# Causal attention in a four-layer kernel: side units of the first stage issued behind the next probability-value piece

## The reference, cut to what matters

```
x = x + attn(layernorm(x))              # x: 8 batches x 1024 tokens x 256
q, k, v = x @ Wq, x @ Wk, x @ Wv        # 16 heads of 16 columns
scores = where(causal, q k^T, -inf) / sqrt(256)
out = softmax(scores) @ v               # per batch and head
```

## Time and profile before

| what | us |
|---|---|
| median of 3 runs (lowest, highest) | 4321.05 (4316.38, 4322.92) |
| the profiled execution, its own time | 4314.35 |
| its span in the trace | 4312.6 |
| PE busy | 4047.0 (94%) |
| DVE busy | 2816.3 (65%) |
| ACT busy | 2658.4 (62%) |
| POOL busy | 1553.8 (36%) |
| the steps of causal attention, from the first score piece on | 85.4 to 1282.1 of the span |

### The profile page before, as it was taken

How to read it: one execution, slowest core, us unless ns; L and a number is a source line. 1 busy time by engine, 2 the same in 40 slices (tenths; PEclk the granted TensorE clock), 3 DMA queues, 4 the chain that set the end, 5 groups by cost and what they waited for, 6 DMA issues and landing times. The chain is left out here.

```text
span 4312.6 us, 65428 instructions
## 1 busy us (share of the span) xinstructions
PE 4047.0 (94%) x23476; PEld 2363.6 (55%) x23476; DVE 2816.3 (65%) x5635; ACT 2658.4 (62%) x3262; POOL 1553.8 (36%) x1303
## 2 busy tenths in 40 slices
PE   7999999999986999999999989997999999999999
PEld 4445444444535787887878765554344444444443
DVE  6777777777747878787887845444554554554553
ACT  2555555555566545455554524443888888888888
POOL 3122122222224535344444411110445445445445
PEclk7999999999998999999999999998999999999999
DMA  7334333433403242323323220002676676676673
GB/s 176 94 96 96 90 87 80 111 81 89 103 25 114 59 117 60 104 73 91 86 78 99 72 65 1 1 1 54 152 164 156 141 164 155 141 164 155 141 164 91
DMA packets 205761, 429.96 MB, mean 100 GB/s; under 512 B 47585, under 2 KB 72561, under 8 KB 189057
## 3 DMA queue, kind: packets, MB, share of 16 engines
q1 hardware_dynamic: 193360, 411.56, 39.6%
q0 software_dynamic: 4160, 6.35, 0.6%
q10 hardware_dynamic: 7920, 7.87, 0.6%
HBM read 338.59 MB, written 87.03 MB: 99 GB/s over the span
## 5 line engine op out<-in xcount | busy, mean ns | idle before, releaser
L2240 ACT ACTIVATE gelu_out<-hidden,b_col 128x1024 f32<-128x1024 f32 x1024 | 1084.4, 1112 | 163.0 <-PE hidden L2140 162.3
L2222 POOL TENSOR_TENSOR combined<-combined,gated 128x512 f32<-128x512 f32 x480 | 619.6, 1291 | 663.7 <-DVE gated L2337 455.1
L705 DVE TENSOR_REDUCE maxima<-front 128x1 f32<-128x512 f32 (+3 forms) x1280 | 737.7, 631 | 172.4 <-PE front L513 98.8
L605 ACT ACTIVATE probsT<-scoresT 128x1024 f32<-128x1024 f32 (+3 forms) x768 | 585.5, 811 | 297.8 <-PE scoresT L541 294.2
L1169 POOL TENSOR_TENSOR pair_sums<-sims 128x1024 f32<-128x1024 f32 x256 | 483.3, 1905 | 665.9 <-DVEq L1301 412.3
L2337 DVE SCALAR_TENSOR_TENSOR gated<-expert_out,b_col,gates_spread 128x512 f32<-128x512 f32 x480 | 360.1, 750 | 502.0 <-PE expert_out L2150 296.2
L2140 PE MATMUL hidden<-slice_stack,w_stack 128*128 128x512 f32 x2048 | 627.0, 428 | 15.0 <-ACT gelu_out L2240 15.0
L2150 PE MATMUL expert_out<-gelu_out,w_sb 128*32 128x512 f32 x4096 | 548.2, 607 | 24.4 <-DVE gated L2337 13.5
L2140 PEld LDWEIGHTS hidden<-slice_stack,w_stack 128*128 128x128 f32 x2048 | 352.0, 189 | 371.0 <-ACT gelu_out L2240 282.2
L1097 PE MATMUL dense<-xnT,dense_weights 128*128 128x512 f32 x2304 | 536.3, 394 | 13.7 <-ACT silu_down L1203 9.3
L450 POOL TENSOR_SCALAR_AFFINE_SELECT probsT<-probsT 128x512 f32<-128x512 f32 x256 | 167.0, 655 | 957.8 <-ACT probsT L605 956.3
(11 more groups left out here) (205 smaller groups left out, 5164.0 us busy)
## 6 DMA issues: line engine op xcount, KB each, us to landing
gates_spread<-gate_scratch SPq DMA_DIRECT2D x512, 256.0 KB, 4.9
dense_weights<-dense_scratch SPq DMA_DIRECT2D x384, 256.0 KB, 2.9
stack_scratch<-split_parts SPq DMA_DIRECT2D x192, 256.0 KB, 3.1
slice_stack<-slice_scratch SPq DMA_DIRECT2D x128, 256.0 KB, 7.9
q_stack<-stack_scratch SPq DMA_DIRECT2D x64, 384.0 KB, 6.2
k_stack<-stack_scratch SPq DMA_DIRECT2D x64, 384.0 KB, 9.3
slice_scratch<-slice_parts SPq DMA_DIRECT2D x32, 512.0 KB, 6.3
out_x<-x_tiles ACTq DMA_DIRECT2D x15, 512.0 KB, 5.0
```

The costliest lines, as they stand in the source:

```text
L605: nc.scalar.activation(PT[:, i % NPT, 2 * pr:2 * pr + 2, at:BANK], ST[pr][:, :, at:BANK], ACT.Exp, scale=SCALE).then_inc(probs_ready, 1)
L705: nc.vector.tensor_reduce(dst, F[k % 3][:, 0:parts * w].rearrange("p (a k) -> p a k", a=parts), AX.X, ALU.max)\
L2222: nc.gpsimd.tensor_tensor(CM[:, par, hc, :], CM[:, par, hc, :], Y[:, u % 2, :], ALU.add)\
L2240: nc.scalar.activation(GH[:, k % 4, :, :], HP[k % HPB][:, :, :], ACT.Gelu, bias=b1c[:, u % E:u % E + 1])\
```

## The change

step(n) returns its list through a new function, behind_values. It walks the list and holds back every x, p, w and t until the next v or o has been put out (where an o follows its v directly, until that o); then it puts out what it held, in the same order. The s, v, o and m units keep their sequence. Of the 2688 units in ORDER 173 move against the others: 56 x, 56 p, 30 w and 31 t. The bank that a front unit uses follows from its new place.

```diff
-        return out + [u for pair in pairs[k:] for u in pair]
+        return behind_values(out) + [u for pair in pairs[k:] for u in pair]
+
+    def behind_values(units):
+
+        out, held = [], []
+        for u, after in zip(units, units[1:] + [None]):
+            if u[0] in "xpwt":
+                held.append(u)
+            else:
+                out.append(u)
+            if u[0] in "vo" and (after is None or after[0] != "o"):
+                out, held = out + held, []
+        return out + held
```

## The result

The changed kernel takes 4391.49 us (median of 4 runs, 4387.95 to 4400.69) where the kernel before takes 4319.68 in the same comparison: ratio 1.0174, 95% interval 1.0162 to 1.0186, 71.8 us slower. The forecast was 4336 with a range to 4355. The direction was right, the size five times too small.

A forecast was written before the change was run, and what follows sets the result against it. PE was taken to set the pace, with PE and DVE waiting for each other through three front banks. Terms for waits summed to +14.6 us on the 4321.05 median, giving 4335.7 (forecast 4336), range 4311 to 4355.

The forecast's parts named there:

- the sum's first sentence: For the whole stage: no matmul, copy or DMA is added or removed, so only waits count; they sum to +14.6 us.
- the first rival: Dense PE work pays: v and moved units run on end, lower-clock stretches go, -16.2 us, 4304.9; chance 0.16.
- the second value unit of an odd step: Eight maxima reductions now run in one row, so the next group starts +0.2 us later in each of seven, +1.4.
- The first value unit of an odd step: Beside DVE's output chain: next group 0.85 us later at seven places, +5.9; statistics in steps 3 and 5, +1.2.
- Even-step value units: Two units of an even step move from amid maxima to amid maxima: taken at 0, bounds -0.8 and +0.8.
- Step 0: Both value units move behind ten maxima in a row: the odd step's price twice, rounded, +1.6 us.
- Projections: With the next step's turned maxima: maxima behind a moved projection wait for its bank, net 1.75 us a pair, +12.2.
- Transposes of x: Four waits in an even step shrink behind a v, the first gets a new one: -0.9 net, seven steps, -6.3.
- Turned maxima: At fourteen step starts the wait ahead goes, but DVE's two operations delay maxima and an o: -0.1 each, -1.4.
- The stacks: Rival: stacks' loads land too late for the maxima reading them, slower still, 4350 with 2 us in each step; chance 0.05.
- the banks: Rival of no change: three rotating banks hide a projection's emptying, its term is 0, 4323.4 us; chance 0.22.
- What would show it: Signs in the changed profile: maxima's weight loads wait on DVE over 176.1 us, v-to-v near 5.9, stage about 1211 us.

The follow-up runs named there:

- e1: Against the kernel before, only the projections move behind the next v: 4346.10 us, ratio 1.0069.
- e4: Against the kernel before, only the transposes of the row maxima (turned maxima) move behind the next v: 4327.36 us, ratio 1.0018.
- e9: Against the kernel before, only the second value unit of each odd step moves behind the next v: 4333.03 us, ratio 1.0033.
- e6: Against the kernel before, only the first value unit of each odd step moves behind the next v: 4329.75 us, ratio 1.0025.
- e2: Against the kernel before, only the value units move behind the next v: 4358.85 us, ratio 1.0096.
- e7: Against the kernel before, only the projections move, to just ahead of the next v instead of behind it: 4317.05 us, ratio 0.9999.
- e3: Against the kernel before, only the transposes of x move behind the next v: 4315.71 us, ratio 0.9997.
- e15: e9's order, with DVE's statistics moved to value units or projections, up to four in a row: 4309.24 us, ratio 0.9985 against the kernel before.
- e5: e2 plus the same value unit computed again, unread, at each of the 30 vacated places: 4372.30 us, ratio 1.0127 against the kernel before.
- e10: Order of the kernel before, but DVE takes each statistic behind one row maximum instead of four or eight in a row: 4327.73 us, ratio 1.0023.

## Why the prediction was right in direction and wrong in size

- **The step that failed is the sum's first sentence**, that nothing is added and "the sum is of waits that come and go". About half of the loss isn't waiting: of the 68.5 us that steps 1 to 14 lost, 31.0 are PE's idle time and 37.5 PE's longer busy time. I read the half-clock stretches only as something to win (the first rival), and gave no term a price for losing clock. The upper end, 4355, was built from the terms' own bounds and so couldn't hold it. The trace of before had an example in step 3, shown above: a hole of 1.35 us and the clock at 0.50 right behind it.
- **The waits alone** came out at twice the sum, 31.0 us for 14.6. By PE's idle time in e1 to e4 the projections bring 14.5 (12.2 forecast), the value units 7.5 (8.5 without step 0), x -2.4 (-6.3) and the turned maxima 10.5 (-1.4). The sizes of the first two were about right, and with them the direction, which is no luck; the sign of the last was wrong.
- **The term furthest off in proportion: the second value unit of an odd step**, +1.4 forecast. e9 measures it at +15.9. The wait was right to within what the rows tell; all the rest is clock.
- **The first value unit of an odd step**: +0.85 a step forecast, 0.9 measured (e6); steps 3 and 5 cost about 4 each instead of 1.5, since the 3.06 us hole also takes the clock down.
- **Even-step value units**, taken at 0 with a bound of 0.8: about 14 us by difference (e2 less e6 and e9, with step 0), 11.1 in the trace of e2. The bound was on waits only. Step 0, +1.6 forecast, took as long as before (e2).
- **Projections**: the place worked out in most detail was right, 5.65 us from v to v against 5.89. Alone they cost 15 us of waits (12.2 forecast) and 28.6 in all; in the whole change the groups with projections in step 8, where the clock stays up in both traces, take 2.56 us longer (by the starts of the v's), above the sum of their terms. That the emptying of the bank is the cause of the waits is shown by e7 against e1.
- **Transposes of x**: -6.3 forecast, -1.8 (indistinguishable from none) measured. PE's waits ahead of them shrank as forecast, from 1.6 us in step 8 to 0.9, and PE's idle time of that step fell from 4.01 to 3.35 in e3. The step got only 0.4 shorter (77.2 to 76.8), since PE is also busy a little longer; why is not shown.
- **Turned maxima**: -1.4 forecast, +9.8 measured (e4), 5.6 of it by 0.7 to 0.8 us a pair of undisturbed steps, and in step 1, which takes 5.5 us longer, with 6.8 us of half-clock time. The prediction did name the cause, that DVE's split of the turned maxima delays what follows, and sized it too small: in e4, too, outputs wait 6.8 us for it in steps 1 to 14 (14 times), and value units 2.6.
- **The stacks** weren't late: in steps 1 to 14 maxima wait once each 1.8 and 1.4 us for a load.
- **The rivals**: the banks don't hide the emptying (1.03 us in the rows). Of the first rival the mechanism was real with its sign reversed: issuing v and the moved units on end didn't keep the clock up, it took work away from places where PE waited anyway. The Trainium skill (TensorE: Matmul & The Clock Gate, A second HAM failure mode: psum-queue depth-cycling) describes a kernel in which short idle gaps of PE between groups of matmuls, as it cycles through banks, make the clock go up and down. e9 and e15 agree with it: a hole of 0.66 us with the clock falling behind it, and no fall in five of seven places once the hole is gone. That rule, and not the one on matmuls back to back, was the one to weigh. The kernel before, with a hole of 0.65 us and the full clock, shows that the gap alone does not decide.
- **What would show it**, as put on record: the weight loads of maxima should have waited longer than 176.1 us on DVE's reductions and subtractions. In the stage they wait 165.5 and 19.5, 185.0 together, but 176.1 and 11.9, 188.0, before: that sign compared unlike sums and was wrong, though PE's waiting grew. PE's idle time per stretch is the better reading. And neither of the two findings that were to prove the prediction wrong (a free bank behind a projection, a shorter stage) could have shown a loss of clock.

## What to carry to other kernels

Before a unit of matmuls is moved, look at what it covers where it stands: a unit that needs no slow engine, beside a place where PE waits for one, fills the time and keeps the clock up, and moving it can cost ten times the wait that one reckons (e9: 1.4 forecast, 15.9 measured). Compare PE's busy time, not only its waits: the same matmuls taking longer at a granted clock of 0.50 is a loss that no list of waits shows. And when a hole of PE comes from a slow engine's side work, move that work under a unit that doesn't need the engine: here that won 12.8 us without touching PE's list.

## What the runs showed of the hardware that I had not expected

- A hole of 0.65 us left the clock at full rate with a value unit of 2.05 us right behind it, and was followed by 3.4 or 6.8 us at 0.50 in all seven odd steps with four maxima and a v there instead (e9).
- What the lower clock costs: PE's busy time grew 37.5 us for 61.4 us more at 0.50 in the changed kernel, 15.9 for 27.3 in e9, about 0.6 each. In e9 the steps grew by 14.7 in all, 0.54 of the 27.3, as PE's idle time fell by 1.2.
- Some 60 us of matmuls for nothing, put into the vacated places, cost 13.5 us (e5), mostly for the clock that they kept (PE's idle time fell by only 4.3 us against e2).
- Less idle time of PE is no proof of less time: in steps 1 to 14 e10 has 38.0 us idle against 41.4, and takes 6.1 us longer.
